# A CIN recommendation tower on one core: stores moved to ACT's queue, transposes and gathers moved, two layers summed by ACT from PSUM

## The reference

```python
def _L0_rec_ref(embeddings, W0, W1, W2):
    x0 = embeddings                      # (1024, 32, 16)
    xk = x0
    outs = []
    for W in (W0, W1, W2):               # 64 outputs each
        xk = jax.nn.relu(jnp.einsum('bmd,bhd,mhk->bkd', x0, xk, W))
        outs.append(jnp.sum(xk, axis=2))
    return jnp.concatenate(outs, axis=1)
...
z = _L0_rec_ref(e, L0_rec_W0, L0_rec_W1, L0_rec_W2)
h = jnp.concatenate([z.reshape(z.shape[0], -1), dense_ctx], axis=1)
h = jnp.maximum(h @ W_top1 + b_top1, 0.0)
h = jnp.maximum(h @ W_top2 + b_top2, 0.0)
y = h @ W_top3
```

## Time and profile before

| | |
|---|---|
| median of 3 runs | 660.86 us (655.26 to 666.55) |
| the profiled execution | 658.72 us, its span 656.9 us |
| busy share of the span | PE 87%, DVE 85%, POOL 70%, ACT 49% |
| granted clock of PE, mean | 0.98 |
| HBM | 147.60 MB read, 232 GB/s over the span |

### The profile page before, as it was taken

One profiled execution on the slowest core, in us unless ns is written; L12 is line 12 of the kernel. 1 busy time (PEld: TensorE's weight loads), 2 busy tenths in 40 slices (PEclk: granted clock), 3 DMA queues, 4 the chain that ended last, 5 costly groups with the idle time before them and its releaser, 6 DMA issues.

```text
span 656.9 us, 7762 instructions
## 1 busy us (share of the span) xinstructions
PE 569.1 (87%) x2620; PEld 205.7 (31%) x2620; DVE 560.9 (85%) x245; ACT 321.3 (49%) x1333; POOL 458.2 (70%) x353
## 2 busy tenths in 40 slices
PE   0379698979999898989898989999998989897996
PEld 0145232323233333323232323333333323232332
DVE  0379799989899999999999999999999999989300
ACT  0224446434736556564736363736556565606121
POOL 6776578878598787888887979788888883444000
PEclk9989799979989999999999999999999999999999
DMA  3858785758577685858484867777685848444000
GB/s 98 271 174 320 289 335 210 275 188 306 232 277 293 240 330 194 303 220 329 176 326 184 310 245 278 293 278 292 238 331 192 342 182 339 163 177 89 1 0 0
DMA packets 29586, 153.03 MB, mean 233 GB/s; under 512 B 7487, under 2 KB 17579, under 8 KB 20971
## 3 DMA queue, kind: packets, MB, share of 16 engines
q1 hardware_dynamic: 19659, 149.11, 59.0%
q0 software_dynamic: 8192, 2.11, 2.5%
q10 hardware_dynamic: 1696, 1.32, 0.7%
HBM read 147.60 MB, written 4.92 MB: 232 GB/s over the span
## 4 chain that ended last, share of the span: by engine, by line
PE 44%; DVE 28%; issue 11%; DMA 9%; ACT 4%; POOL 3%; SPq 0%; POOLq 0%; DVEq 0%
PE acc L587 39%; DVE prod L427 25%; DMA spread<-x_scratch 4%; ACT x L490 4%; DMA x_scratch<-xt 2%; POOL rows L376 2%; PE x L660 2%; PE x L649 1%; DVE z L440 1%; POOL prod_pool L389 1%; DMA x_scratch_half<-xt 1%; DVE xt L416 1%; DMA rows<-table,ids_sb 1%; PE x L666 1%; PE x L653 0%
## 5 line engine op out<-in xcount | busy, mean ns | idle before, releaser
L427 DVE TENSOR_TENSOR prod<-spread,x 128x4096 f32<-128x4096 f32 (+3 forms) x190 | 532.5, 2862 | 36.6 <-issue 11.8
L587 PE MATMUL acc<-prod,w 128*64 128x512 f32 (+1 forms) x2076 | 449.6, 581 | 79.8 <-DVE prod L427 79.8
L376 POOL DMA_INDIRECT rows<-table,ids_sb x256 | 243.2, 950 | 76.8 <-issue 70.0
L587 PEld LDWEIGHTS acc<-prod,w 128*64 128x64 f32 x2076 | 160.4, 141 | 358.7 <-issue 320.2
L389 POOL TENSOR_TENSOR prod_pool<-spread,x_pool 128x1024 f32<-128x1024 f32 (+1 forms) x93 | 214.8, 2341 | 67.6 <-ACT x_pool L490 67.4
L490 ACT ACTIVATE x<-acc 64x512 f32<-64x512 f32 (+1 forms) x136 | 74.1, 545 | 88.4 <-PE acc L587 87.1
L506 ACT ACTIVATE relu_out<-acc 128x512 f32<-128x512 f32 (+1 forms) x51 | 29.2, 573 | 150.5 <-PE acc L587 149.6
L498 ACT ACTIVATE relu_out<-relu_out 128x16 f32<-128x16 f32 x480 | 95.3, 200 | 0.5
L587 PE MATMUL acc<-prod_pool,w 128*64 128x512 f32 (+1 forms) x372 | 89.8, 585 | 0.0
L498 ACT ACTIVATION_READ_ACCUMULATOR relu_out<-relu_out 128x1 f32 x480 | 89.8, 187 | 0.0
L490 ACT ACTIVATE x_pool<-acc 64x512 f32<-64x512 f32 (+1 forms) x136 | 77.1, 567 | 2.0
(11 more groups left out here) (21 smaller groups left out, 26.0 us busy)
## 6 DMA issues: line engine op xcount, KB each, us to landing
spread<-x_scratch SPq DMA_DIRECT2D x60, 2048.0 KB, 8.5
first<-x_scratch SPq DMA_DIRECT2D x15, 512.0 KB, 3.7
spread<-x_scratch_half SPq DMA_DIRECT2D x7, 1024.0 KB, 6.2
rows<-table,ids_sb POOLq DMA_INDIRECT x256
x_scratch<-xt SPq DMA_DIRECT2D x15, 256.0 KB
w<-w ACTq DMA_DIRECT2D x2, 512.0 KB, 5.3
spread<-x_scratch_half SPq DMA_DIRECT2D x4, 256.0 KB, 3.9
spread<-wt SPq DMA_DIRECT2D x2, 384.0 KB, 4.7
```

The lines of the kernel that those rows point to most:

```text
L376: nc.gpsimd.indirect_dma_start(rows[u % 2][:, j * D:(j + 1) * D], None, table, bass.IndirectOffsetOnAxis(ap=index, axis=0)).then_inc(gathe ...
L427: nc.vector.tensor_tensor(prod[:, at:at + count, 0:n], tiles(u, t, count), x[:, 0:n].rearrange("p (a n) -> p a n", a=1).to_broadcast([P, c ...
L587: last = nc.tensor.matmul(parts(to[K * blk:K * blk + K, 0:n]), w, side(moving[:, 0:2 * n], blk), start=start, stop=stop)
```

## The change

Five things are done.

- **Stores.** SP no longer issues them, except the first part of unit 0's. ACT does, on its own queue: `stores(u + 2)` stands in `after_2(u)` behind the relu of layer 2 (for units 1 and 2 in `after_1`), and waits for the transpose.
- **Transposes.** `turn(u + 2)` moves from between steps 2 and 3 of layer 3 to the place ahead of the wait for `x2` (from loop 1 on).
- **Gathers.** POOL now issues the last 9 gathers of unit u+2 and the first 2 of unit u+3 ahead of layer 3's products, and 5 more of unit u+3 behind them.
- **Sums.** ACT sums layers 1 and 3 straight out of the bank with 32 activations (relu, accumulator), and the bank is free when the last is done. DVE sums layer 2 alone, and layer 3 of the last unit.
- **Layer 3's end.** Step 3 (tiles 12 to 15) becomes two steps of two tiles. The places in the ring follow from the new steps: layer 1's products, for instance, now wait until PE is done with tile 10 of the layer 2 ahead (tile 4 before).

Two smaller things go with them: `x1_pool` and `x2_pool` are not written for the three half-unit layers in which POOL has no tiles, and SP's wait ahead of group 1 is for the new last step.

The diff, cut to its core:

```diff
-    return (0, 4), (4, second), (8, 4), (12, 4)
+    return (0, 4), (4, second), (8, 4), (12, 2), (14, 2)
...
-AHEAD = 5
+EARLY = 2
+AHEAD = 7
...
             for u in range(LAST):
-                sp.wait_ge(turned, u + 2)
-                store(sp, u + 1)
                 load_first(u + 1)
...
             for u in range(LAST - 1):
                 products(u, 2)
-                if u + 2 < UNITS:
-                    gather(u + 2, slice(AHEAD, fields(u + 2)))
+                gather(u + 2, slice(AHEAD, None))
+                gather(u + 3, slice(0, EARLY))
                 products(u, 3)
-                if u + 3 < UNITS:
-                    gather(u + 3, slice(0, AHEAD))
+                gather(u + 3, slice(EARLY, AHEAD))
...
                 layer_1(u + 1)
-                sum_d(u, 0)
+                if 0 < u and u + 2 < UNITS:
+                    turn(u + 2)
                 dve.wait_ge(x_ready[1], u + 1)
                 if u + 1 < LAST:
                     for i in range(len(steps_of(3, u))):
-                        if i == (2 if u == 0 else 3) and u + 2 < UNITS:
-                            turn(u + 2)
+                        if i == 2 and u == 0:
+                            turn(2)
                         multiply(3, u, i, x2)
                         if i == 2:
-                            sum_d(u, 1)
+                            sum_2(u)
...
+            def sum_kept(u, layer, src):
+                if u:
+                    act.wait_ge(summed[layer], u)
+                n = width(u) // 2
+                per_b = src[:, 0:n].rearrange("p (c b e) -> p b c e", c=4, e=D // 4)
+                to = relu_out[layer][:, 0:n].rearrange("p (b c e) -> p b c e", c=4, e=D // 4)
+                for b in range(samples(u)):
+                    last = nc.scalar.activation(to[:, b, :, :], per_b[:, b, :, :], ACT.Relu,
+                                                accum_out=z[:, layer, z_at(u) + b:z_at(u) + b + 1])
+                last.then_inc(summed[layer], 1)
...
+            def stores(u):
+                act.wait_ge(turned, u + 1)
+                store(act, u)
+                store_wrapped(act, u)
...
                 spread_out(u, x1, src).then_inc(x_ready[0], 1)
-                spread_out(u, x1_pool, src).then_inc(x_pool_ready[0], 1)
-                keep(u, 0, src)
+                if u < 2:
+                    stores(u + 1)
+                if pool_tiles(2, u):
+                    spread_out(u, x1_pool, src).then_inc(x_pool_ready[0], 1)
+                sum_kept(u, 0, src)
...
+                nc.scalar.activation(relu_out[1][:, 0:n], src[:, 0:n], ACT.Relu).then_inc(relu_2_ready, 1)
+                if 0 < u and u + 2 < UNITS:
+                    stores(u + 2)
...
-                    pe.wait_ge(relu_ready[before[0] - 1], before[1] + 1)
+                    pe.wait_ge((summed[0], relu_2_ready, summed[2])[before[0] - 1], before[1] + 1)
```

More of the change, by code:

```diff
@@ L79, in order_of @@
                 ("step", 3), ("step", 4), ("step", 5)]
-    return [("step", 0), ("step", 1), ("pool", 0), ("pool", 1), ("step", 2), ("pool", 2), ("step", 3)]
+    return [("step", 0), ("step", 1), ("pool", 0), ("pool", 1), ("step", 2), ("pool", 2), ("step", 3),
+            ("step", 4)]
 CUT = 2
-CUT_ORDER = ([("step", 0), ("step", 1), ("pool", 0), ("pool", 1), ("pool", 2)], [("step", 2), ("step", 3)])
+CUT_ORDER = ([("step", 0), ("step", 1), ("pool", 0), ("pool", 1), ("pool", 2)], [("step", 2), ("step", 3), ("step", 4)])
 def sequence():
@@ L147, in made, with pool_units @@
     return PLACES[layer, u, i % len(steps_of(layer, u))][0] + 1
+def pool_units(layer, u):
+    return sum(1 for v in range(u + 1) if pool_tiles(layer, v))
 def used(layer, u):
@@ L235, in build @@
         x_pool_ready = [sem(f"x{l + 1}_pool_ready") for l in range(2)]
-        relu_ready = [sem(f"relu_ready{l}") for l in range(3)]
+        relu_2_ready, relu_last_ready = sem("relu_2_ready"), sem("relu_last_ready")
         summed = [sem(f"summed{l}") for l in range(3)]
@@ L278, in store, with store_wrapped @@
             engine.dma_start(to, src.to_broadcast([P, 2, n])).then_inc(scratch_in[u % 2], 16)
+        def store_wrapped(engine, u):
+            n = width(u) // 4
             to = scratch(u, 2 * M)
@@ L341, in _ @@
                 if u >= 1:
-                    sp.wait_ge(prod_ready, made(3, u - 1, 3))
+                    sp.wait_ge(prod_ready, made(3, u - 1))
                 load_group(u + 1, 1)
@@ L370, in gather @@
             def gather(u, part):
+                if u >= UNITS:
+                    return
                 if part.start == 0 and u >= 2:
@@ L382, in products @@
                 if pool_tiles(layer, u):
-                    pool.wait_ge(x_pool_ready[layer - 2], u + 1)
+                    pool.wait_ge(x_pool_ready[layer - 2], pool_units(layer, u))
                 for i, t in enumerate(pool_tiles(layer, u)):
@@ L480, in _ @@
                 if i == 1:
-                    sum_d(LAST, 1)
-            sum_d(LAST, 2)
+                    sum_2(LAST)
+            dve.wait_ge(relu_last_ready, 1)
+            sum_d(LAST, 2, relu_out[2])
         @block.scalar
@@ L533, in after_2 @@
                     squares(1)
-                spread_out(u, x2_pool_of(u), src).then_inc(x_pool_ready[1], 1)
-                keep(u, 1, src)
+                if pool_tiles(3, u):
+                    spread_out(u, x2_pool_of(u), src).then_inc(x_pool_ready[1], 1)
+                if u:
+                    act.wait_ge(summed[1], u)
+                n = width(u) // 2
+                nc.scalar.activation(relu_out[1][:, 0:n], src[:, 0:n], ACT.Relu).then_inc(relu_2_ready, 1)
+                if 0 < u and u + 2 < UNITS:
+                    stores(u + 2)
             def after_3(u):
                 act.wait_ge(prod_free, used(3, u))
-                keep(u, 2, acc[BANKS[3, u][0]])
+                src = acc[BANKS[3, u][0]]
+                if u < LAST:
+                    sum_kept(u, 2, src)
+                else:
+                    act.wait_ge(summed[2], LAST)
+                    nc.scalar.activation(relu_out[2][:, :], src[:, :], ACT.Relu).then_inc(relu_last_ready, 1)
             act.dma_start(w_1[:, :, :], w1a).then_inc(consts_in, 16)
```

17 lines of the change are left out of this document (8 added, 9 removed).

## The result

The changed kernel takes 667.4 us (median of 20 runs, 665.03 to 671.97). The kernel before, run beside it, takes 665.3 us (median of 20 runs, 655.26 to 676.7). The ratio is 1.0094, 95% interval 1.007 to 1.0117: slower by about 0.9%. The time lies in the range, 8.8 us above the forecast, and the sign of the small difference is wrong: forecast -2.2 us, measured +6.2 (0.0094 of 661).

A forecast was written before the change was run, and what follows sets the result against it. The longest loop through the engines was taken as the bound. Terms -4.3 - 0.5 - 0.6 + 1.5 + 1.7 = -2.2 us turned 658.72 into 656.5; 2.1 us for the median gave 658.6 us, range 645 to 674.

The forecast's parts named there:

- DVE alone: In the middle, with layer 1's sum gone, DVE's own work would take 33.9 us a unit.
- the moved transpose: Ahead of layer 3 it waits for gathers, so a long unit takes 35.84 us from step 0 to step 0.
- PE's loop: In the middle, PE's 32 tiles plus its start and ACT's spread would take 34.64 us a unit.
- two-unit loop: In the middle, a long unit waiting for gathers is followed by a short one: 70.48 us, 35.24 a unit.
- rival of the late landing: In the middle, gathers land in 4.21 us, beside loads: period 36.64 us, time 675.4 us; chance 0.14.
- ACT's sums: For layer 1, a pair out of PSUM costs 0.20 us, leaving 3.2 us before PE wants the bank.
- bank rival: ACT holds layer 1's bank too long, at 0.39 us a pair: 37.4 us a unit, time 691 us; chance 0.06.
- In the head: At unit 2, the longer bank hold against earlier stores and loads: from -4.1 to +4.1 us, +1.5 taken.
- Stores: Issued some 8 us earlier in the unit, with first loads following; worth nothing in the middle.
- the rival's reason: Stores land no sooner, so the early units' 5.1 us stay and the time is 664 us; chance 0.07.
- The clock: Behind PE's hole ahead of layer 3 in six long units, falls cost 0 to 10.2 us; one, 1.7, taken.
- rival without a wait: In the middle, gathers land in time and PE's 34.64 us is the period: 648.2 us; chance 0.28.

The follow-up runs named there:

- both cures: The changed kernel with gathers shifted by four in place of two and layer 3 beginning with 2 + 2 tiles: 646.1 us, ratio 0.9752 to the kernel before.
- e4_stores_sp: The changed kernel with the stores back on SP's queue, behind the loads as before: 672.5 us.
- e3_sums_only: The kernel before with only ACT's sums out of PSUM for layers 1 and 3 and the split of layer 3's last step: 664.0 us.
- e1_shift4: The changed kernel with the gathers shifted by four in place of two: 656.2 us.

## Why the prediction went wrong, step by step

*DVE alone, PE, the moved transpose: right.* DVE alone, 33.9 us, is 34.1 in the kernel with both cures, where it is the bound (34.33 less 0.21). PE's loop of 34.64 us is the measured period once nothing else binds (shift of four). The two-unit loop with the wait for gathers is right too, in each of its parts (2.47, 30.37 and 1.44 us), and its dependence on the gathers' place was borne out at 0, 2, 3 and 4. Landing stayed quick, so the rival of the late landing fell; only at 466.64 did a unit wait 3.32 us, 3.0 us after its last gather's end (463.62). These landings are counted from the end of POOL's issue, as in the forecast; from the start of the issue the shown one takes 2.38 us (354.37 to 356.75), so 1.42 is not the figure to set beside the cost of a whole DMA.

*ACT's sums: right in the middle, where a pair was taken at 0.20 us and took 0.16.* The bank rival fell. In the head the hole is there as foreseen, 3.18 us, and the net at unit 2 was +0.2 (103.45 for 103.24) where +1.5 was taken. The hold of the bank in the tail, 1.57 us, was put at nothing.

*Stores: right as far as the runs show.* SP's wait went and the loads are in time, so the rival's reason did not come. That its 5.1 us are also the distance of e4_stores_sp from the changed kernel is not to be leaned on, since the two did not run side by side.

*The clock: this step failed.* I gave its bounds as 0 to 10.2 us for six long units, and took one fall, 1.7, without a reason for the one. From unit 2 to 13 there were seven, of 14.2 us, above even the upper bound. Their rows take 14.2 us more than seven times 4.51 us (1.70 + 2.83 + 1.70 + 1.70 + 1.60 + 1.70 + 2.98). Four of them, 8.0 us, stand in units that waited for gathers; three, 6.2 us, do not, and for those the forecast had no term at all. Unit 2 to unit 14 takes 437.1 us, 14.2 over the six two-unit loops of 422.9; that the two agree so closely is partly chance, as short units can take up a part of a fall, and one landing was late. Against the forecast's own sum, 656.5 us, the profiled execution is 11.8 longer: -1.3 in the head, +12.5 in the middle (14.2 less the one fall in the sum), +0.6 in the tail (0.5 gained where 1.1 was taken).

What value the rows allowed is less plain. I predicted that the hole would reach 2.2 us, and both holes shown, of 4.12 and 1.58 us, had a fall behind them. But PE's timeline of the kernel before has holes as near to 2.2 us with full clock behind them:

```profile
218.39 4.51 PE L587 MATMUL acc<-prod,w 128*64 128x512 f32 x20 [1.71 <-DVE prod L427]
...
593.36 3.65 PE L587 MATMUL acc<-prod,w 128*64 128x512 f32 x16 [2.38 <-DVE prod L427]
```

So the trace gave neither one fall nor six, only the range. A fall in each long unit would have given 8.5 us more, 667.1 us, close to the measured 667.4 partly by luck, since three of the seven falls came elsewhere. I counted falls by how rare they had been; the change made long holes ahead of layer 3 regular.

*The rival without a wait* became real once two more gathers were moved forward: 648.2 us was its price, and a shift of four gave 651.6 and 656.2.

*The base* played a part too. The median of the first three runs was 660.9 us, that of the 20 beside the changed kernel 665.3, and runs of it reach from 655 to 677 us. Which of them the one profiled execution was, 658.72 us, decides some of the 8.8 us.

## What to carry to other kernels

When a change widens an idle hole of TensorE in every unit, price a fall of the clock for every unit as one end of the range, and do not take a value by how often falls occurred before. Cutting the first step behind a serial dependency in half, so that TensorE starts sooner, was worth 2.0% here, beside 2.7% for removing the wait (ratios of 0.9893 and 0.9826, from 1.0094; their intervals overlap). When a wait is moved ahead of other work, look at once for the last producer it waits for and move that forward by as much: here two gathers further turned 0.9% slower into 1.7% faster.

## What the runs showed that I had not expected

- A hole of 1.88 us ahead of layer 3 was followed by full clock at 326.10 and by half clock at 398.10, in one execution of the changed kernel. In the same execution all seven holes of 2.02 us and more ahead of layer 3, from unit 2 to unit 14, were followed by half clock; in e3_sums_only and e1_shift4 one of 2.52 us was not. Hole size alone does not decide.
- Executions of one kernel can differ by their falls: the two kept of the shift of four, 650.95 and 656.23 us, have mean granted clocks of 0.983 and 0.975, and the falls in units 2 and 3 of the second are 4.6 us. With one hole ahead of layer 3, each fall makes PE late, so that DVE's products of layer 1 are ready early and the next unit's idle time again gathers ahead of layer 3; this would explain the runs of falls in e3_sums_only, but it is argued from the rows and no run isolates it.
- Activations with an accumulator read follow each other every 0.16 us out of PSUM, and every 0.20 us in place in SBUF.
